# VectorE weighs and adds the outputs of the first expert layer straight out of PSUM, and TensorE gets constant products in some twenty more waits

## The reference

```python
# _L0_ffn_ref: x is (4, 512, 128), 8 experts, width and hidden width 128
gate = jnp.einsum('btd,edi->beti', x, Wg)
up = jnp.einsum('btd,edi->beti', x, Wu)
h = jax.nn.silu(gate) * up
e_out = jnp.einsum('beti,eid->betd', h, Wd)
out = jnp.einsum('bte,betd->btd', weights, e_out)
# _L0_attn_ref: 16 heads of 8, 64 landmarks
SV = kernel1 @ iterative_inv(kernel2) @ (kernel3 @ v)
# the block
x = x + 0.5 * _L0_ffn_ref(_layernorm(x), ...)
x = x + _L0_attn_ref(_layernorm(x), ...)
x = x + 0.5 * _L0_ffn_ref(_layernorm(x), ...)
x = x + 0.5 * _L1_ffn_ref(_layernorm(x), ...)
x = x + _L1_attn_ref(_layernorm(x), ...)
x = x + 0.5 * _L1_ffn_ref(_layernorm(x), ...)
```

## Time and profile before

| what | value |
|---|---|
| median of three launches | 877.46 us (875.3 to 881.89) |
| the profiled execution | 880.06 us, its span 878.6 us |
| busy | PE 724.0, PEld 556.0, DVE 530.4, ACT 401.5, POOL 446.0 us |
| mean granted clock of TensorE | 0.931 of full speed |
| call 1, its 32 steps | 15 to 102 us |
| attn0, scores and inverse's end | 251 to 306 us |
| call 2 and the shared expert | 318 to 473 us |
| first routed stage, attn1, second routed stage | 473 to 607, 607 to about 731, 731 to 878 us |

### The profile page before, as it was taken

One profiled execution on the slowest core, in us unless ns is written; L12 is line 12 of the kernel. 1 busy time (PEld: TensorE's weight loads), 2 busy tenths in 40 slices (PEclk: granted clock), 3 DMA queues, 4 the chain that ended last, 5 costly groups with the idle time before them and its releaser, 6 DMA issues.

```text
span 878.6 us, 19350 instructions
## 1 busy us (share of the span) xinstructions
PE 724.0 (82%) x6670; PEld 556.0 (63%) x6670; DVE 530.4 (60%) x1596; ACT 401.5 (46%) x971; POOL 446.0 (51%) x489
## 2 busy tenths in 40 slices
PE   7889998889999898888998677875888987788830
PEld 6778856569977567777776455553666774555520
DVE  6975596558856287867782354443876662354524
ACT  3657654556425455455413355640554323455520
POOL 4755530435500046375673367775357771477770
PEclk9999998999978998899999999997998998899985
DMA  9999999480045091011111444425001112344417
GB/s 229 214 216 217 217 214 219 97 160 4 5 101 111 1 324 37 1 46 37 44 56 52 107 105 109 107 79 209 1 31 54 56 57 50 86 109 111 111 52 245
DMA packets 121024, 93.98 MB, mean 107 GB/s; under 512 B 14176, under 2 KB 111840, under 8 KB 120544
## 3 DMA queue, kind: packets, MB, share of 16 engines
q1 hardware_dynamic: 104256, 70.00, 36.1%
q0 software_dynamic: 9216, 19.68, 6.5%
q10 hardware_dynamic: 7456, 3.07, 1.7%
HBM read 31.76 MB, written 57.41 MB: 101 GB/s over the span
## 4 chain that ended last, share of the span: by engine, by line
PE 39%; POOL 16%; DVE 15%; issue 12%; SPq 9%; ACT 5%; DMA 4%; ACTq 1%; DVEq 0%; POOLq 0%
POOL sorted_rows L455 8%; SPq L713 7%; POOL expert_rows L731 7%; PE banks L1939 5%; PE banks L1324 4%; PE banks L404 2%; PE banks L405 2%; PE banks L406 2%; PE banks L916 2%; DVE hT L1237 2%; PE banks L642 1%; PE banks L176 1%; PE banks L1956 1%; PE banks L1900 1%; DVE rows_x L215 1%
## 5 line engine op out<-in xcount | busy, mean ns | idle before, releaser
L731 POOL DMA_INDIRECT expert_rows<-y,goal x160 | 153.2, 957 | 103.9 <-DVE y L854 55.7
L455 POOL DMA_INDIRECT sorted_rows<-rows_x,row_of x128 | 126.4, 987 | 67.2 <-issue 37.2
L1196 ACT ACTIVATE ys<-banks,wtab 128x128 f32<-128x128 f32 x256 | 73.1, 370 | 65.2 <-PE banks L1324 53.5
L916 PE MATMUL banks<-routed_w,t 128*64 x320 | 83.0, 403 | 11.0 <-issue 5.5
L404 PE MATMUL banks<-x_high,w_high 128*128 128x512 f32 x192 | 86.1, 449 | 0.4 <-POOL w_low L1075 0.4
L1324 PE MATMUL banks<-w,hT 128*128 128x128 f32 x512 | 75.2, 293 | 11.1 <-DVE hT L1237 10.9
L916 PE MATMUL banks<-routed_scratch,t 128*64 128x256 f32 x320 | 83.1, 403 | 0.0
L1122 POOL TENSOR_TENSOR x<-ys,x 128x512 f32<-128x512 f32 x43 | 55.5, 1290 | 54.3 <-ACT ys L1196 54.0
L1324 PEld LDWEIGHTS banks<-w,hT 128*128 128x128 f32 x512 | 69.0, 203 | 20.2 <-DVE hT L1237 17.7
L406 PE MATMUL banks<-x_high,w_low 128*128 128x512 f32 x192 | 77.6, 404 | 0.0
L405 PE MATMUL banks<-x_low,w_high 128*128 128x512 f32 x192 | 77.1, 402 | 0.0
(11 more groups left out here) (342 smaller groups left out, 1720.4 us busy)
## 6 DMA issues: line engine op xcount, KB each, us to landing
sorted_rows<-zeros SPq DMA_DIRECT2D x32, 1120.0 KB, 17.3
tile<-sorted_rows SPq DMA_DIRECT2D x252, 35.0 KB, 2.0
routed_w<-in_ffn_w SPq DMA_DIRECT2D x8, 768.0 KB, 11.4
w<-in_ffn_w SPq DMA_DIRECT2D x20, 192.0 KB, 5.6
expert_rows<-y,goal POOLq DMA_INDIRECT x160
tile<-sorted_rows ACTq DMA_DIRECT2D x68, 35.0 KB
qS<-x_high SPq DMA_DIRECT2D x8, 256.0 KB, 6.5
sorted_rows<-rows_x,row_of POOLq DMA_INDIRECT x128
```

The lines of the kernel that those rows point to most:

```text
L455: POOL.indirect_dma_start(sorted_rows, bass.IndirectOffsetOnAxis(self.row_of[:, g, i:i + 1], 0), rows_x[:, 4 * g + i // TOPK, :], None).th ...
L731: POOL.indirect_dma_start(expert_rows, bass.IndirectOffsetOnAxis(goal[:, 4 * q + i:4 * q + i + 1], 0), y[q % 6][:, i * P:(i + 1) * P], Non ...
L916: last = PE.matmul(pairs(q)[ROWS * h:ROWS * h + ROWS, i, :], t[q % 2][:, rows], weights(q, i, h, slice(0, 2 * P)), start=True, stop=True)
L1196: last = SCL.mul(ys[s % 2][:, j * P:(j + 1) * P], bank[4 + s % 2][:, j * P:(j + 1) * P], wtab[:, t, e:e + 1])
```

## The change

Six edits:

1. ScalarE's `scale`, the tiles `ys`, the signal `scaled_done` and `add` go. VectorE gets `weigh_and_add(s - 1)` in step s, behind the pieces of the routing table and ahead of statistics and normalised rows: four SCALAR_TENSOR_TENSOR of 128x128, bank times weight plus x, into x. `down(s)` and the first products of the next stages wait for `added` instead.
2. In call 1, `following` normalises group 0 at offset 6 (before 4), transposes it at 8 (5) and copies at 9 (6).
3. `transposes` waits for its PSUM bank first and for the rows last, with constant products between: 2 for group 3 of call 2's own norm, 0, 2, 1 and 1 for the groups of `srt`.
4. attn0: `landmark_values` multiplies all 72 columns in place of 8, the pairs in reversed order so that later ones overwrite what is not wanted; three constant products around the second `turn_maxima`, and one each ahead of the last `spread1` and `output`.
5. The routed stage, both times: 3 more products behind the wait for the first rows, 2 within the first transposes, 3 and 2 ahead of the waits for quads 2 and 3.
6. attn1: 22 products in place of 10 ahead of the wait for the rows that come back, and 3 ahead of the last group's transposes.

That is 5 constant products more in attn0, 6 in call 2, 15 in attn1 and 10 in each routed stage, 46 in all. The signals, allocations and indices that follow from the edits are left out of the diff.

```diff
@@ Norm
-            def transposes(self, g):
-                PE.wait_ge(*xn_ready(self.first + g + 1))
+            def transposes(self, g, meanwhile=0):
                 if self.turn[g]:
                     PE.wait_ge(*xT_ready(self.turn[g]))
+                keep_busy(meanwhile, bank[6])
+                PE.wait_ge(*xn_ready(self.first + g + 1))
@@ routed stage
                     PE.wait_ge(*dispatched(4 * TOPK * NG))
-                    keep_busy(2, bank[0])
+                    keep_busy(5, bank[0])
                     PE.wait_ge(*loaded(0))
                     transposes(0, range(2))
+                    keep_busy(2, bank[2])
...
+                    keep_busy(3, bank[1])
                     PE.wait_ge(*loaded(2))
...
+                        if n == 2:
+                            keep_busy(2, bank[1])
@@ first expert layer
-            FOLLOWING = dict(statistics=1, normalised=4, transposes=5, copy=6)
+            FOLLOWING = [dict(statistics=1, normalised=6, transposes=8, copy=9)] + [dict(statistics=1, normalised=4, transposes=5, copy=6)] * 2
@@ its GpSimd
-                for s in range(POOL_ADDS):
+                for s in range(rows if srt else STEPS):
...
-                    add(POOL, s)
@@ its ScalarE
-                    if 0 < s <= STEPS:
-                        scale(s - 1)
...
-                if not srt:
-                    scale(STEPS - 1)
@@ its VectorE
+                def weigh_and_add(s):
+
+                    g, e = divmod(s, rows)
+                    if s in (0, rows, 2 * rows):
+                        DVE.wait_ge(*wtab_ready(g + 1))
+                    DVE.wait_ge(*down_done(s + 1))
+                    if e:
+                        DVE.wait_ge(*added(s))
+                    for j in range(4):
+                        t = 4 * g + j
+                        last = DVE.scalar_tensor_tensor(out=x[:, t, :], in0=bank[4 + s % 2][:, j * P:(j + 1) * P], scalar=wtab[:, t, e:e + 1],
+                                                        in1=x[:, t, :], op0=ALU.mult, op1=ALU.add)
+                    last.then_inc(*added.inc)
...
                     for n, piece in routed_at.get(s, ()):
                         assert next(routes[n]) == piece
+                    if 0 < s <= STEPS:
+                        weigh_and_add(s - 1)
                     if s in statistics_at:
...
-                    if POOL_ADDS < s <= STEPS:
-                        add(DVE, s - 1)
@@ its TensorE
                     if s > 1:
-                        PE.wait_ge(*scaled_done(s - 1))
+                        PE.wait_ge(*added(s - 1))
...
-                        norm.transposes(transposes_at[s])
+                        norm.transposes(transposes_at[s], 2 if srt and transposes_at[s] == 3 else 0)
...
-                        srt.norm.transposes(g)
+                        srt.norm.transposes(g, (0, 2, 1, 1)[g])
@@ attn0
-                    for k in range(NK):
+                    for k in reversed(range(NK)):
                         for r in HALF:
-                            c = b * GH * 2 + k * HD
-                            last = PE.matmul(bank[5][r, c:c + HD], K[b][r, k, :], A[b][r, k, M:TC], start=True, stop=True)
+                            c = ((B - 1 - b) * NK + k) * HD
+                            last = PE.matmul(bank[5][r, c:c + TC], K[b][r, k, :], A[b][r, k, :], start=True, stop=True)
...
+                keep_busy(1, bank[6])
                 turn_maxima(0, 1)
+                keep_busy(2, bank[6])
...
+                    if b == B:
+                        keep_busy(1, bank[0])
                     if b:
                         spread1(b - 1)
...
+                    if b == B:
+                        keep_busy(1, bank[0])
                     if b:
                         output(b - 1)
@@ attn1
-                keep_busy(10, bank[5])
+                keep_busy(22, bank[5])
                 PE.wait_ge(*earlier.back_here[0])
...
+                        keep_busy(3, bank[5])
                         srt.norm.transposes(LAST)
```

More of the change, by code:

```diff
@@ L639, in tensor_down @@
                 elif e == 0 and self.first:
-                    PE.wait_ge(*scaled_done(self.first - 1 + g))
+                    PE.wait_ge(*added(self.first - 1 + g))
                 for j in range(4):
@@ L1109, in groups_at @@
                 return [g for g in range(NG) if srt and s == rows * (g + 1) + (srt.SPREAD if g in (1, 2) else srt.SOON)[piece]]
-            FOLLOWING = dict(statistics=1, normalised=4, transposes=5, copy=6)
+            FOLLOWING = [dict(statistics=1, normalised=6, transposes=8, copy=9)] + [dict(statistics=1, normalised=4, transposes=5, copy=6)] * 2
             def following_at(s, piece):
-                return [g for g in range(NG - 1) if following and s == rows * (g + 1) + FOLLOWING[piece]]
-            def add(engine, s):
-                g = s // rows
-                xg = x[:, 4 * g:4 * g + 4, :]
-                engine.wait_ge(*scaled_done(s + 1))
-                if s % rows:
-                    engine.wait_ge(*added(s))
-                engine.tensor_tensor(xg, ys[s % 2][:, :].rearrange("p (j d) -> p j d", d=D), xg, ALU.add).then_inc(*added.inc)
+                return [g for g in range(NG - 1) if following and s == rows * (g + 1) + FOLLOWING[g][piece]]
             def sync_engine():
@@ L1185, in scalar_engine @@
                     high_part(fresh[3], 3)
-                def scale(s):
-                    g, e = divmod(s, rows)
-                    if s in (0, rows, 2 * rows):
-                        SCL.wait_ge(*wtab_ready(g + 1))
-                    SCL.wait_ge(*down_done(s + 1))
-                    if s > 1:
-                        SCL.wait_ge(*added(s - 1))
-                    for j in range(4):
-                        t = 4 * g + j
-                        last = SCL.mul(ys[s % 2][:, j * P:(j + 1) * P], bank[4 + s % 2][:, j * P:(j + 1) * P], wtab[:, t, e:e + 1])
-                    last.then_inc(*scaled_done.inc)
                 for s in range(steps):
@@ L1297, in vector_engine @@
                 else:
-                    add(DVE, STEPS - 1)
+                    weigh_and_add(STEPS - 1)
             def tensor_engine():
@@ L1371, in ffn0 @@
             wtab_ready.ends(3)
-            scaled_done.ends(STEPS)
             added.ends(STEPS)
```

16 lines of the change are left out of this document (7 added, 9 removed).

## The result

The changed kernel takes 886.22 us (median of four launches, 885.88 to 887.38) where the kernel before takes 876.38 (four, 873.93 to 881.89): ratio 1.0106, 95% interval 1.0055 to 1.0156. It is slower by about 1%, where the forecast was 865 us, and outside the range of 856 to 876. The profiled execution took 886.14 us, its span 884.9, 6.3 us more than the span before.

The account below looks back on a forecast made before the run. Bound by stage: neither engine full early in call 1, then TensorE; TensorE at half speed in attn0; both well filled in call 2. Terms -2.3 - 3.6 - 0.5 - 5 - 1 = -12.4 took 880.06 to 867.7, median-adjusted 865 us; range 856 to 876.

Parts of the forecast that it names:

- The price of weighing: Both calls: the four weighing instructions take 0.82 us of VectorE a step, estimated from 0.98 us for 64 rows.
- rival B: Weighing: VectorE's four don't overlap, 0.28 us each instead of 0.20; +5 to +12, so 870 to 877 us; chance 0.10.
- The sign of being wrong: Weighing: the forecast is wrong if the four instructions together take over 1.2 us.
- GpSimd's stretch: Call 1, 15 to 62 us: without GpSimd's adds, VectorE's lengthened rows give back some 7 us.
- -2.3 in my sum: Call 1: waits shrink before 62 us, nothing gained after; -2.3 us, range -5 to +1.
- Call 2: Call 2: fewer half-clock drops and less VectorE time; -5 us, range -12 to +3.
- mostly past: Call 2: VectorE's 7.7 us wait for `ys` becomes one for `down_done`, a step later than ScalarE's, mostly past.
- the half clock of the scores: attn0, 251.7 to 268.6 us: 72 columns and constant products keep full clock; -3.6 us, range -5.5 to -1.
- my two terms: attn0: -3.6 us for the stretch at 1.2 GHz and -0.5 us at its end.
- The second routed stage: Second routed stage: products fill waits around TensorE's half-clock first transposes; -1 us, range -2.5 to 0.
- C: VectorE's queue becomes the bound once its work in a step exceeds 2.30 us; about 897 us; chance 0.08.
- A: attn0 and call 2: the constants don't hold the clock, drops only move; 874 us, 871 against the median; chance 0.20.

Follow-up runs that it names:

- Experiment 5: Changed kernel with one 512-column weighing instruction instead of four of 128, leaving out three of four routing weights: 1032.32 us, ratio 0.9998 to the kernel before.
- Experiment 4: Kernel before with all adds on VectorE, one of 512 columns a step, none on GpSimd, ScalarE still scaling: 874.96 us, ratio 0.9964.
- experiment 2: Kernel before with all the constant products and 72-column landmark values, weighing and adding as before, group 0 at its old steps: 870.83 us, ratio 0.9957.
- experiments 1: Kernel before with only the weighing and adding moved to VectorE, no new constant products, eight-column landmark values, group 0 at old steps: 892.25 us, ratio 1.0195.
- experiment 7: Changed kernel with one more constant product in each of three waits of attn0's first part: 1041.92 us, ratio 1.0100 to the kernel before.
- experiments 3: Changed kernel with weighing moved behind the pieces of sorting and the norm's statistics, rows and split in each step: 878.66 us, ratio 1.0021 to the kernel before.
- 9: Changed kernel with the later weighing and three more constant products in attn0's first part: 1033.36 us, ratio 1.0019 to the kernel before.
- 8: Changed kernel with the following norm's group 0 back at its old steps in call 1: 1045.05 us, ratio 1.0131 to the kernel before.
- 6: Kernel before with 512-column adds on VectorE, all the constant products and 72-column landmark values: 1030.05 us, ratio 0.9977.
- experiment 12: Kernel before with 512-column adds on VectorE, all constant products, 72-column landmark values and three more products in attn0's first part, measured again: 866.27 us, ratio 0.9880.

## Why the prediction was wrong

**The price of weighing** is the step that failed first. I took 0.82 us of VectorE for the four, from a run of the same operation over 64 rows that lasts 0.98, less a tail. It is 1.05, and the run 1.12, just what the four of L215 last in the same group of rows; I had set that row aside as rival B. The sign of being wrong that I had named, fours of over 1.2 us, was set too high to show this. Experiment 5 shows what the difference of price does where VectorE is full: four becoming one take 0.39 us less, and call 1's first 16 steps are 0.39 us shorter each. The Trainium skill's page "VectorE: DVE Perf Modes", in its section on the TRN2 errata, was the better guide: 120 cycles and one an element for a source in PSUM give, an estimate, 1.03 us for four of 128 and 0.66 for one of 512, and the traces have 1.05 and 0.66 from start to start. I had let it count in a third of the steps only.

**GpSimd's stretch** was sized well. By the lengths of the single instructions in the first 16 steps, 16 of `hidden` in both, VectorE's other work than the weighing fell from 50.4 to 43.4 us: 7.0 came back, where I had counted 7 for 15 steps. But the sum behind it was added up wrongly: 50.4 less 7, 1.2 and 0.1 is 42.1, not 43 to 45. Over the 16 steps the trace has 51.26 us in place of 42.91, and the 60 weighing instructions hold 16.8 of them (60 of 256 by 71.9). Experiment 4, where the adds cost 10.3 us and the stretch goes too, is 2.5 us shorter in these steps. The price of four instructions ate this relief: the length came out as -2.3 in my sum and +2.7 in the trace.

**Call 2** (-5 forecast, +5.9 measured) is the second step that failed, at the sentence that VectorE's new wait for `down_done` was "mostly past". I had named the mechanism for a rival, that the four stand ahead of other pieces, but priced only VectorE's sum of work and never looked whether TensorE's own order holds a wait for one of these pieces ahead of the `down` that VectorE waits for. It does, at each rank product. Moving the weighing behind these pieces took 8.0 us out of call 2 up to the last 32 transfers (109.3 against 117.3). A lower price alone took 6.5 out of its first part, and the order alone 5.3 of the same part; each brings it back to about the 56.4 us of the kernel before, so the two are not to be added. Two counts of the working were off besides: VectorE had 20 of call 2's 32 adds, not 21 (one of the earlier trace rows is call 1's), and the trace has four stretches of half clock in call 2 up to 429.48 us, not five.

**Attn0.** The step on the half clock of the scores was right: the stretch that ran at 1.2 GHz has a clock of 1.00, in experiment 2 too. Which part of the edit does it, the 72 columns or the three constant products beside them, no run separates. From the end of its first part (166.4 against 157.8 us) to call 2, 160.3 us became 156.2, -4.1, the sum of my two terms. But I had taken the first part as untouched, and it took 5.7 us more there: 0.8 up to the piece shown above (33.5 us before, 34.3 after), where the last group's rows came 0.6 us late, and 4.9 by a half clock of 20.5 us instead of 6.8. Nothing in its order had changed. The wait ahead of the fall is the same 1.38 us in both; in experiments 1 and 2, with the same wait, there was no fall at all. Of the nine kernels without the three products seven have a fall in this part in their profile, of the five with them none, though the products leave the first wait at 1.28 to 1.29 us. That speaks for the products, but how they act isn't known, and with one profile for each kernel chance isn't ruled out. Nor is it shown that the fall accounts for 5 us of the changed kernel's median: its four launches lie within 1.5 us of each other, which speaks for it, while experiment 7 has the changed kernel's ratio, and experiments 3 and 9 have equal ratios in spite of 9 us between their profiles' attn0. Since the profile of 3 is its slowest launch, part of that gap may be this launch's own. This stays open.

**The rest.** The second routed stage gained 2.6 us up to the end of the span, forecast -1; the first 1.3, forecast 0; attn1's -0.2 was forecast as 0, where only the wait was to be filled. In experiment 2, with the same products, the three are -2.2, +0.9 and +2.2 us, so only the gain of the second stage comes twice.

**The rivals.** B had the right price and the wrong size (870 to 877), since it put it on the path in 15 to 40 steps and on top of gains that call 2 didn't give. C had the right mechanism, a queue that becomes the bound, with a price that wasn't needed: it decided at 1.05 us a step, not 1.64. A didn't hold: in experiment 2 attn0 has no half clock and call 2 up to the last 32 transfers one stretch of 3.4 us, where the kernel before has four. (A's step of +6.3 should have been +6.6: 3.6, 1 and 2.) Put together, the differences between trace and forecast are +5 in call 1, +5.7 in attn0, +10.9 in call 2, -1.3, -0.2 and -1.6 behind: 18.5 of the 18.7 us between -12.4 and +6.3.

## What to carry to other kernels

Price an operation by the nearest row in shape on all 128 rows, and compare four short instructions with one long one by the start-to-start distance; here the difference was 0.39 us a step in call 1's first 16, more than the whole edit brings there at the lower price (52.1 to 48.9 us, 0.2 a step). When an operation with a wait is put on an in-order engine, look at what stands behind it there and who waits for that, and whether the awaited engine holds one of those waits ahead of the work awaited: in call 2 its place behind these pieces was worth about as much as its price. Ask whether a relief (GpSimd's adds away from VectorE's rows) can be had without the costly part: here the adds alone, at 512 columns, gave it.

## What the runs showed of the hardware

- The same 228 or so records of attn0's first part ran with no half clock (experiments 1 and 2) or with 6.8, 13.7, 20.5 or 30.8 us of it (before; 4 and 5; changed and 8; 3 and 6), with the same first wait of 1.38 us and at start times a few us apart. A short wait that nothing follows in one kernel is followed by 20 us at 1.2 GHz in another. With one constant product behind each of three of these waits there was none in five profiles.
- Two chips take 1032 us for a program that takes 876 to 878 on the others. The parts up to call 2's first transfer of sorted rows are the same within some 2 us; from the first to the last of the first routed stage's 80 transfers it takes 148 to 154 us in place of 109 to 112. GpSimd is busy with them for 76.6 us on such a chip (experiment 5) and 76.8 on the other kind (experiment 12), so it is the waits between them that grow. Why isn't known from these runs.
